# Decoder layer on one core: weights made stationary in the expert tiles, row numbers kept for four tiles instead of eight, and the final joins moved to GpSimd

## What is computed

```
x = layernorm(x + attention(x))            # 16 heads, causal
x = layernorm(x + cross_attention(x, ctx)) # with decay
x = layernorm(x + ffn(x))
# ffn: one shared expert, and 2 of 8 routed experts for each row
hs = x @ sw1 + sb1;  shared = (silu(hs[:256]) * hs[256:]) @ sw2 + sb2
probs = softmax(x @ gate_w + gate_b);  top 2 of 8
routed = sum over the two of p_e * ((silu(h[:256]) * h[256:]) @ rw2[e] + rb2[e]),  h = x @ rw1[e] + rb1[e]
```

## Time and profile before

| | us |
|---|---|
| median of 3 runs (762.58 to 775.45) | 767.11 |
| profiled execution | 767.07 |
| its span (first to last instruction) | 765.0 |
| of which tile stage, about 473 to 698 | 225 |
| of which end, about 698 to 765 | 67 |

### The profile page before, as it was taken

How to read it: one execution, slowest core, us unless ns; L and a number is a source line. 1 busy time by engine, 2 the same in 40 slices (tenths; PEclk the granted TensorE clock), 3 DMA queues, 4 the chain that set the end, 5 groups by cost and what they waited for, 6 DMA issues and landing times.

```text
span 765.0 us, 19153 instructions
## 1 busy us (share of the span) xinstructions
PE 704.2 (92%) x5464; PEld 531.8 (70%) x5465; DVE 476.4 (62%) x1435; ACT 449.7 (59%) x1242; POOL 375.1 (49%) x524
## 2 busy tenths in 40 slices
PE   6977899899999999999997897899999999999973
PEld 5866788788888888888875554556565556665542
DVE  2545588788888889888866545344444444443575
ACT  0267788788888888888862221445444444453225
POOL 1001134235445545544545471577777777777212
PEclk9998999999999999999999999999999999999987
DMA  8743564523233323323454257545555555554963
GB/s 292 259 150 105 188 220 146 196 64 93 71 86 91 76 86 100 111 78 102 123 157 160 72 195 205 131 82 86 85 83 88 84 83 83 83 88 59 300 228 138
DMA packets 84778, 97.97 MB, mean 128 GB/s; under 512 B 12160, under 2 KB 76288, under 8 KB 83680
## 3 DMA queue, kind: packets, MB, share of 16 engines
q1 hardware_dynamic: 59728, 64.03, 27.5%
q0 software_dynamic: 14752, 23.53, 15.6%
q10 hardware_dynamic: 10224, 9.49, 4.7%
HBM read 55.90 MB, written 41.10 MB: 127 GB/s over the span
## 4 chain that ended last, share of the span: by engine, by line
PE 66%; DMA 7%; DVE 7%; issue 7%; SPq 6%; POOL 4%; ACT 2%; ACTq 1%; POOLq 0%; DVEq 0%
PE ps L1014 12%; PE ps L1023 6%; PE ps L777 6%; PE ps L874 4%; PE ps L765 4%; PE ps L742 4%; PE ps L787 4%; PE ps L745 3%; PE ps L898 3%; PE ps L877 3%; POOL total L666 3%; PE ps L817 3%; DMA attn_only<-in_ctx 2%; PE ps L1000 2%; PE ps L797 2%
## 5 line engine op out<-in xcount | busy, mean ns | idle before, releaser
L1089 ACT ACTIVATE prob<-ps,nmax 128x128 f32<-128x128 f32 x512 | 146.9, 379 | 29.6 <-DVE nmax L1288 29.6
L1014 PE MATMUL ps<-first_use,xgT 128*128 x284 | 133.8, 593 | 1.5 <-ACT xgT L1207 1.5
L666 POOL DMA_INDIRECT total<-rot,result_row x71 | 112.1, 1579 | 14.1 <-issue 12.8
L1549 DVE TENSOR_TENSOR tile_parts<-ps,attn_only 128x512 f32<-128x512 f32 x71 | 49.1, 692 | 90.0 <-PE ps L1014 90.0
L1288 DVE TENSOR_REDUCE nmax<-ps 128x4 f32<-128x512 f32 x128 | 82.2, 685 | 23.7 <-PE ps L765 22.7
L599 POOL TENSOR_TENSOR rot<-products 128x128 f32<-128x128 f32 x128 | 61.1, 498 | 64.9 <-DVE products L1298 64.7
L1096 ACT COPY pT<-ps 128x512 f32<-128x512 f32 x128 | 76.9, 601 | 20.6 <-PE ps L777 14.4
L777 PE MATMUL ps<-tf,prob 128*128 128x128 f32 x512 | 80.0, 280 | 6.1 <-ACT pT L1096 6.1
L623 POOL DMA_INDIRECT sent<-packets,pos x64 | 63.4, 990 | 36.9 <-PE ps L765 22.6
L1014 PEld LDWEIGHTS ps<-first_use,xgT 128*128 128x128 f32 x284 | 53.5, 190 | 40.1 <-issue 36.5
L650 POOL TENSOR_TENSOR tile_parts<-tile_parts 128x256 f32<-128x256 f32 x71 | 51.1, 720 | 57.2 <-ACT tile_parts L1202 57.2
(11 more groups left out here) (140 smaller groups left out, 1443.2 us busy)
## 6 DMA issues: line engine op xcount, KB each, us to landing
xg<-sent ACTq DMA_DIRECT2D x68, 130.5 KB, 2.1
first_use<-total SPq DMA_DIRECT2D x12, 512.0 KB, 8.6
total<-zeros POOLq DMA_DIRECT2D x1, 4224.0 KB, 17.9
k_dram<-first_use SPq DMA_DIRECT2D x4, 1024.0 KB, 4.4
attn_only<-in_x_turned SPq DMA_DIRECT2D x32, 128.0 KB, 3.2
attn_only<-k_dram SPq DMA_DIRECT2D x256, 16.0 KB
attn_only<-in_x SPq DMA_DIRECT2D x32, 128.0 KB, 2.9
attn_only<-in_ctx SPq DMA_DIRECT2D x32, 128.0 KB, 2.8
```

The costliest lines, as they stand in the source:

```text
L666: eng.indirect_dma_start(totals[slot % 2], bass.IndirectOffsetOnAxis(ap=result_row[:, slot:slot + 1], axis=0), yw[:, slot % 4, :], None, c ...
L1014: mm = eng.matmul(ps[:, r, :], xgT[:, r, c, :], rw1_sb[:, bass.ds(e * (DC * 2 * FFN) + c * 2 * FFN, 2 * FFN)], start=(c == 0), stop=(c == ...
L1089: ins = eng.activation(prob[:, t % 2, 4 * u + n, :], SCORE[u][:, n * P:(n + 1) * P], ACT.Exp, bias=nmax[:, t % 2, 4 * u + n:4 * u + n + 1])
L1549: eng.tensor_tensor(hid[:, r, :], ps[:, r, :], rb_h[:, bass.ds(e * (2 * FFN), 2 * FFN)], ALU.add).then_inc(hid_set, 1)
```

## The change

In the tiles:

- `hidden` is turned round: 128x128 blocks of the first weights are stationary and `xgT` streams past in 128 columns, 8 products instead of 2. The hidden values come out turned, so `turn_h`, its copy and GpSimd's product go. The bias is one number for each partition now: ScalarE takes silu straight from PSUM with it (2 x 128 columns), and VectorE adds the bias and multiplies in one instruction (`gated`, 2 x 128 columns).
- The stationary weights have fixed addresses: for each tile the expert's first weights are copied into one of two buffers `w_now`, one half by ScalarE (`weights_first`) and one by VectorE (`weights_second`), each two tiles ahead. VectorE copies the tile's biases too (`bias_of`).
- `result` of tile i-1 instead of i-2 comes in step i; `weighted` stays two tiles behind.
- The loads of `xg` go from ScalarE to SP.
- `result_row` has four columns instead of eight, and all loops have four tiles.
- GpSimd's order in a tile is: wait for the weighted rows, `tile_weight` of the tile two ahead, scatter.

At the end: `join` goes from VectorE to GpSimd, between its `root`s, and VectorE's order changes. The table of biases `rb1` is loaded at the start (16 KB); eight loads of 256 KB fall away.

```
@@ rows and buffers
-        result_row = sb("result_row", [P, 8], U32)
+        result_row = sb("result_row", [P, 4], U32)
@@ VectorE, tiles
+            def weights_second(i, r, e):
+                after(eng, hid_made, 2 * i - 2)
+                eng.tensor_copy(w_now[:, r, 1, :], rw1_sb[:, bass.ds(e * (DC * 2 * FFN) + 2 * FFN, 2 * FFN)]
+                                ).then_inc(w_second_set, 1)
             def rows_of(i, slot, added):
                 after(eng, row_added[slot % 2], 16 * added)
-                eng.tensor_copy(result_row[:, slot:slot + 1], xg[:, slot % 4, D:D + 1]).then_inc(packet_row, 1)
+                eng.tensor_copy(result_row[:, slot:slot + 1], xg[:, slot, D:D + 1]).then_inc(packet_row, 1)
+            def tiles(k, many=4):
...
+                    for f in range(FFN // P):
+                        gated(i, n % 2, f)
+                    if not (first and n == 0):
+                        out_y(i - 1, (n - 1) % 2, read[n - 1])
+                    if not ends:
+                        bias_of(i + 1, (n + 1) % 2, read[n + 1])
+                        weight_parts(i + 1, (n + 1) % 4, k + 1 + (n + 1) // 4)
+                        rows_of(i + 1, (n + 1) % 4, 2 * k + (n - 1) // 2)
+                    if not last or n + 2 < many:
+                        read[n + 2] = expert(i + 2)
+                        weights_second(i + 2, n % 2, read[n + 2])
@@ TensorE, tiles
+            def hidden(i, r):
                 eng.wait_ge(xgT_set, i + 1)
+                eng.wait_ge(w_first_set, i + 1)
+                eng.wait_ge(w_second_set, i + 1)
+                after(eng, gh_set, 2 * i - 2)
+                for half in range(2):
+                    for f in range(FFN // P):
+                        cols = half * FFN + f * P
+                        for c in range(DC):
+                            mm = eng.matmul(ps[:, 2 * r + half, f * P:(f + 1) * P],
+                                            w_now[:, r, c, cols:cols + P],
+                                            xgT[:, r, c, :], start=(c == 0), stop=(c == DC - 1))
@@ ScalarE, tiles
+                    silu(i, n % 2, 0)
+                    silu(i, n % 2, 1)
+                    if not ends:
                         out_x(i + 1, (n + 1) % 2)
+                    if not last or n + 2 < many:
+                        weights_first(i + 2, n % 2, expert(i + 2))
                     if not (first and n < 2):
+                        weighted(i - 2, n % 2, (n - 2) % 4, 2 * k + n // 2 - 2)
@@ GpSimd, tiles and end
+                    wait_rows(i, n % 2, 2 * k + n // 2)
+                    tile_weight(i + 2, (n + 2) % 4)
+                    add_rows(n)
...
+            def join(q):
+                eng.wait_ge(fin_in[q], 32)
+                rows = fin[:, q * QB:(q + 1) * QB, :]
+                eng.tensor_tensor(rows, rows, odd_of(q), ALU.add).then_inc(joined, 1)
+            join(0)
+            join(1)
+            root(0)
+            join(2)
+            root(1)
+            join(3)
+            root(2)
+            join(4)
+            join(5)
+            root(3)
...
```

More of the change, by code:

```diff
@@ L698, in root @@
                 eng.tensor_tensor(rstd3[:, q, :], var3[:, q, :], neg_half[:, :], ALU.pow).then_inc(rstd3_set, 1)
-            for q in range(NQ):
-                root(q)
+            def join(q):
[12 more added lines that the diff above has]
+            root(3)
+            join(6)
+            root(4)
+            join(7)
+            root(5)
+            root(6)
+            root(7)
         @block.tensor
@@ L1568, in expert, with tiles @@
                 return eng.value_load(tile_expert[0:1, bass.ds(i, 1)], min_val=0, max_val=NE - 1)
[L1570 to L1572 removed]
+            def tiles(k, many=4):
+                first, last = isinstance(k, int) and k == 0, isinstance(k, int) and k == TILES // 4
+                read = {}
                 for n in range(many):
[L1574 to L1584 removed]
+                    i = 4 * k + n
+                    ends = last and n == many - 1
+                    for j in (n - 1, n + 1):
+                        if j not in read and not (first and j < 0) and not (last and j == many):
+                            read[j] = expert(4 * k + j)
+                    for f in range(FFN // P):
+                        gated(i, n % 2, f)
+                    if not (first and n == 0):
+                        out_y(i - 1, (n - 1) % 2, read[n - 1])
[6 more added lines that the diff above has]
+                        weights_second(i + 2, n % 2, read[n + 2])
@@ L1586, in _ @@
+            for i in range(2):
+                weights_second(i, i, expert(i))
+            bias_of(0, 0, expert(0))
+            weight_parts(0, 0, 1)
+            rows_of(0, 0, 0)
             tiles(0)
-            with eng.Fori(1, TILES // 8) as k:
+            with eng.Fori(1, TILES // 4) as k:
                 tiles(k)
-            two_before, before = tiles(TILES // 8, TILES % 8)
-            out_y(TILES - 2, TILES % 2, two_before)
-            out_y(TILES - 1, (TILES - 1) % 2, before)
-            def join(q):
-                eng.wait_ge(fin_in[q], 32)
-                rows = fin[:, q * QB:(q + 1) * QB, :]
-                eng.tensor_tensor(rows, rows, odd_of(q), ALU.add).then_inc(joined, 1)
+            tiles(TILES // 4, TILES % 4)
@@ L1599, in moments @@
+            out_y(TILES - 1, (TILES - 1) % 2, expert(TILES - 1))
             def moments(q):
```

242 lines of the change are left out of this document (97 added, 145 removed).

## The result

The changed kernel takes 793.15 us (median of 6 runs, 790.25 to 797.7), the kernel before 769.38 (median of 6); the ratio is 1.0353, with a 95% interval of 1.0288 to 1.0418. It is 3.5% slower. A ratio here, as in all that follows, is that of the means of the undisturbed runs of a comparison: two runs of the kernel before, 775.45 and 4014.01 us, are not in this one, which is why it is not 793.15 / 769.38. The profiled execution of the changed kernel has a span of 790.0 us, against 765.0.

What follows compares the result with a forecast made beforehand. TensorE bound the tiles before, not the end; after the change a loop through the scatter's landing would. 767.07 + 26.4 (tiles) + 0.6 (start) - 1.5 (last tiles) - 4 (joins) = 788.6, said as 788 us, range 766 to 803.

Steps and rivals of the forecast that it cites:

- The step on the loop: Tiles: row numbers wait for the scatter three tiles back, the weights copy queues behind; 10.36 us per three tiles; chance 0.60.
- The copy of weights: VectorE's 128x512 float32 copy `weights_second` in the tiles: 0.67 us taken, between 0.14 and 0.69.
- The size of a tile: Tile stage: 3.50 us a tile, 0.40 more than before, from about the fifth tile on; 66 tiles, +26.4 us.
- the head of VectorE's loop: One step in four, with branch and two expert reads ahead of `gated`: 3.7 us between `hidden` starts instead of 3.45.
- The upper ends of the sum: Tiles, loop through the scatter with every term at its upper end: 10.9 us for three tiles, 3.63 each.
- TensorE's floor: TensorE's own work in a tile: 2.90 us, 2.95 with a small gap, 0.15 below the kernel before.
- the rival that TensorE still binds: Tiles: row numbers do not wait, the whole loop takes under 8.85 us; 752 us, at best 748; chance 0.10.
- rival 4: Tiles: clock falls with TensorE 83% busy, up to +20, 808 us, or weight loads do not fit; chance 0.10.
- the first tiles: Start of the tile stage: no scatter to wait for yet, so 0 us of change.
- The joins: End of kernel: joins on GpSimd at 2.3 us each, last gate about 745 instead of 748.69; -4 us (-6 to +3).
- The last tiles: Last tile has no turn, copy and product behind `hidden`: -1.5 us (0 to -2.5).
- The start: Start of kernel: one more small DMA on SP ahead of the first store of keys, +0.6 us.

Runs made afterwards that it cites:

- cols8: Changed kernel with eight columns of row numbers instead of four, VectorE's and GpSimd's loops of eight tiles: 750.02 us, ratio 0.971 to the kernel before.
- cols5: Changed kernel with five columns of row numbers instead of four, VectorE's and GpSimd's tile loops written out: 750.23 us, ratio 0.976 to the kernel before.
- order_unroll: Changed kernel, four columns, with VectorE's copy of weights ahead of the row numbers and its loop written out: 747.13 us, ratio 0.975 to the kernel before.
- unroll: Changed kernel, four columns and same order, with VectorE's tile loop written out (no branch, one read a tile): 797.6 us, ratio 1.034 to the kernel before.

## Why the prediction was right, and where it was not

**The step on the loop** held. The prediction named four columns, the wait of the row numbers and the copy queued behind it, and the runs bear out each of the three: the loss goes with more columns (`cols8`, `cols5`) and with the copy moved ahead of the wait, once the head of the loop is gone too (`order_unroll`). Term by term, forecast against the rows of `unroll`:

| term | forecast | measured |
|---|---|---|
| `hidden` | 1.82 | 1.89 |
| turn to copy | 0.45 | 0.42 |
| copy to `weights_first` | 0.82 | 0.79 |
| to the weighting | 0.53 | 0.52 |
| weighting to the scatter | 1.11 | 1.41 |
| landing | 3.8 | 3.84 |
| VectorE, landing to copy | 1.0 | 0.76 |
| copy and handover | 0.83 | 0.67 |
| sum | 10.36 | 10.30 |

The sum is right partly because misses cancel. GpSimd sees the weighted rows 0.27 after their end and needs 0.64 from `tile_weight` to the scatter, 0.91 in all, where I had 0.44 to 0.76 and took 0.60. The copy of weights took 0.43, and I had chosen 0.67 from the slope of an addition of two tiles and from a `tensor_scalar` between SBUF tiles, neither of which is a plain copy; the Trainium skill (VectorE: DVE Perf Modes, "The perf-mode tier table"), which gave an estimated 0.42, was right, and the trace agrees with it. By its figure alone the forecast would have been 3.37 a tile, further off: a right term in a sum with other terms too low.

**The size of a tile** was the step that missed: 3.66 instead of 3.50, +35.7 us instead of +26.4. Of the 9.3 us between them, 2.1 lie in the first seven steps, where I had 1.2 us more than before, from the fifth tile on, and it was 3.3: the first scatter landed late, TensorE paused and its clock fell. The other 7.2 are 63 steady steps that got longer by 0.51 instead of 0.40. The loop without a head is 3.48 there, close to the 3.45. It is the head of VectorE's loop that I had too small: it costs 0.17 a tile (3.65 against 3.48) and not 0.06. I had 0.2 for the branch and 2 x 0.7 for the reads, 1.6 from the copy to `gated`; it was 2.22 in the median. The step at the head took 4.06 in the mean, not 3.7, and the step two behind it was long too, at 3.90, where I had said that one in four would be. Why there are two, no run shows. 36 of 63 row numbers waited, 57%, for my "most"; 40 us held 10.9 tiles, for 11.4.

The upper ends of the sum are added up wrongly in the prediction: they make 10.98, so 3.66 a tile, and not 10.9 and 3.63. Nothing in the forecast hangs on it.

**TensorE's floor**: 2.85, for 2.90 to 2.95. `hidden` takes 1.78 when TensorE runs through and 1.88 after a pause. The price given to the rival that TensorE still binds, 748 to 752, looks like what eight columns brought (750.0), the same kernel but for the one wait and half of the branches. The equal numbers are partly luck: by its ratio of 0.971 that version stands at 745 on the 767.07 of the prediction, since the floor was lower and the end gained 9 and not 5.

**The clock** was 1.00 from 520 to 715 us at 87% busy; rival 4 did not come. Only at the start of the stage, behind the 4.0 us in which TensorE waited for the first scatter, was it at the lower level, for about 3.4 us. The prediction had put the first tiles at 0.

**The joins**: 2.34 each (forecast 2.3), -4.8 alone and -6.4 with the tiles (forecast -4, at best -6). Most of the end's gain comes ahead of the last gate: from the last `hidden` to it were 54.1 us before (694.6 to 748.69) and 47.3 now (728.0 to 775.31), and from the gate to the end 16.3 and 14.7. `root` took 1.02. **The last tiles**: -2.0 (forecast -1.5). **The start**: +0.6 was forecast for one more small load; the starts of the runs spread over 18 us, so this can't be said.

The spans add up. The forecast span is 786.5 (788.6 less the 2.1 around the span), the measured one 790.0, 3.5 more: 9.3 more in the tiles, less 3.0 of gain at the end and 2.8 at the start that I had not forecast. So the time came out 5 us from the 788 partly by luck, as the two smaller misses took back 5.8 of the 9.3 us.

## What to carry to other kernels

A ring of buffers that is freed by a DMA's landing closes a loop: count the tiles it spans, add up every handover around it, and compare with the span times the bound engine's own work; here four columns, with the copy of weights behind the wait, meant 10.3 us against 3 x 2.86 and cost 6% (a ratio of 1.035 against 0.971), five meant 10.3 against 4 x 2.86 and cost nothing. On an engine that works in order, put what others wait for ahead of the wait. The idle time before an instruction is no measure of its cost: 68.5 us of it was free in `order_unroll`, where nothing that TensorE was about to need stood behind.

## What the runs showed that was not expected

- A read of a number from SBUF into a register and the work on it occupy VectorE's sequencer for 0.55 to 0.7 us (0.30 for the load, 0.19 for the range, the rest for its steps). In the changed kernel 5 of the 104 loads between 480 and 700 us took 0.58 to 0.65, each the first behind the loop's branch, but ten of the 15 first loads did not. Nothing of it counts as busy time.
- `hidden`, 16 instructions of 128 streaming columns, took 1.78 or 1.88, depending on whether TensorE had paused just before, at the same granted clock of 1.00.
- GpSimd's accumulating scatter lands 3.6 to 4.1 us after its start, in `order_unroll` at 2.9 us a tile; in the changed kernel, at 3.6 us a tile, the row numbers that waited for one came 3.7 to 4.1 after its start in 38 of 39 cases. The exceptions are the first scatters of the stage, 5.8 and 5.9 in `order_unroll` and 6.5 in the changed kernel.
- At the end of a pause of 4.0 us on TensorE, at the start of the tile stage, the granted clock fell to its lower level for 3.4 us, and `hidden` took 3.3 us instead of 1.9.
- Written out, VectorE's loop of 71 tiles ran as fast as or faster than the loop in every pair: 256.0 to 247.6, 208.5 to 202.3, 239.2 to 204.9, 237.4 to 224.1 us.
